# Fused attention and mixture-of-experts kernel: the second scatter of a pair issued without waiting for the first, y held twice, and norm 2 between the two groups of routing scatters

## What is computed

```python
x = alpha * attention_conv(x) + x                      # per image: q, k, v, 1024 x 1024 softmax
t = to_tokens(x)
t = t + proxy_attention(ln(t))                         # cumulative sums over the tokens, 16 proxies
flat = ln(t).reshape(-1, 256)
logits = flat @ gate_w.T                               # (4096, 8)
top_vals, top_idx = top_k(logits, 2)
top_w = softmax(top_vals)
for e in range(8):
    hdn = gelu(flat @ w1[e] + b1[e])                   # (4096, 1024)
    out = out + combine[:, e:e+1] * (hdn @ w2[e] + b2[e])
t = t + out
```

## Time and profile before

| | us |
|---|---|
| median of 3 runs | 944.57 |
| lowest and highest | 942.77, 949.17 |
| the profiled execution | 946.73 |
| its span, first to last instruction | 945.0 |

### The profile page before, as it was taken

The page is one execution under the profiler, slowest core; times in us unless marked ns, Lnnn a source line. Parts: engine busy times, 40 slices in busy tenths (PEclk is TensorE's granted clock), DMA queues, the critical chain, the costliest instruction groups (busy, mean ns, idle before and its releaser), DMA issues.

```text
span 945.0 us, 18862 instructions
## 1 busy us (share of the span) xinstructions
PE 803.9 (85%) x5745; PEld 730.7 (77%) x5746; DVE 481.1 (51%) x1134; ACT 325.0 (34%) x588; POOL 426.8 (45%) x404
## 2 busy tenths in 40 slices
PE   4998789896999999605989989989798986988993
PEld 3888679786566575405989889889798986988993
DVE  4787778685436564332535434544453453444442
ACT  2846557474324342102331332223232323223221
POOL 2564547345115754553435435444444443544422
PEclk9999999998658885656998999989899999999997
DMA  9575765925013231105686676666857777566542
GB/s 305 202 304 195 288 266 162 415 90 225 23 45 67 46 68 51 62 1 179 202 284 205 212 246 190 223 204 217 299 159 240 251 219 263 168 218 195 146 113 24
DMA packets 61043, 171.83 MB, mean 182 GB/s; under 512 B 18017, under 2 KB 48097, under 8 KB 53825
## 3 DMA queue, kind: packets, MB, share of 16 engines
q1 hardware_dynamic: 43632, 146.49, 42.8%
q0 software_dynamic: 16000, 19.48, 11.2%
q10 hardware_dynamic: 1360, 5.24, 1.4%
HBM read 184.23 MB, written 47.78 MB: 246 GB/s over the span
## 4 chain that ended last, share of the span: by engine, by line
DMA 35%; PE 7%; issue 7%; POOL 3%; DVE 1%; POOLq 1%; SPq 0%; DVEq 0%; ACT 0%
DMA out_tok<-y,to_row 34%; PE ps_y L72 2%; PE ps_y L73 2%; PE ps_y L74 2%; POOL x_rows L1184 1%; DVE y L1277 1%; DMA records<-places 1%; PE ps_h L72 1%; PE ps_h L73 1%; PE ps_h L74 1%; POOL out_tok L1190 1%; POOL from_row L1178 0%; POOL to_row L1196 0%; DVE gl L1286 0%; DMA x_rows<-normed,from_row 0%
## 5 line engine op out<-in xcount | busy, mean ns | idle before, releaser
L1239 ACT ACTIVATE g<-ps_h,bias 128x256 f32<-128x256 f32 x288 | 120.7, 471 | 346.7 <-PE ps_h L74 346.7
L72 PE MATMUL ps_y<-wbuf,gl 128*128 x576 | 172.5, 300 | 44.7 <-DVE gl L1286 44.6
L1190 POOL DMA_INDIRECT out_tok<-y,to_row x72 | 120.9, 1679 | 113.9 <-DVE y L1277 77.7
L73 PE MATMUL ps_y<-wbuf,gh 128*128 x576 | 168.9, 293 | 0.0
L74 PE MATMUL ps_y<-wbuf,gh 128*128 x576 | 168.4, 292 | 0.0
L72 PE MATMUL ps_h<-xth,wbuf 128*128 128x256 f32 x576 | 163.2, 283 | 1.4 <-DVE xtl L1263 1.4
L73 PE MATMUL ps_h<-xtl,wbuf 128*128 128x256 f32 x576 | 163.7, 284 | 0.0
L74 PE MATMUL ps_h<-xth,wbuf 128*128 128x256 f32 x576 | 163.0, 283 | 0.0
L72 PEld LDWEIGHTS ps_y<-wbuf,gl 128*128 128x128 f32 x576 | 116.2, 202 | 48.3 <-issue 48.3
L73 PEld LDWEIGHTS ps_y<-wbuf,gh 128*128 128x128 f32 x576 | 116.5, 202 | 0.1
L74 PEld LDWEIGHTS ps_y<-wbuf,gh 128*128 128x128 f32 x576 | 115.9, 201 | 0.0
(11 more groups left out here) (181 smaller groups left out, 1495.3 us busy)
## 6 DMA issues: line engine op xcount, KB each, us to landing
wbuf<-wsplit SPq DMA_DIRECT2D x70, 2048.0 KB, 7.9
wsplit<-wbuf SPq DMA_DIRECT2D x14, 2048.0 KB, 11.4
wraw<-in_w SPq DMA_DIRECT2D x16, 1024.0 KB, 6.5
xraw<-in_x_ch ACTq DMA_DIRECT2D x5, 1024.0 KB, 10.6
tok<-in_x_tok SPq DMA_DIRECT2D x1, 4096.0 KB, 16.9
out_tok<-tok SPq DMA_DIRECT2D x8, 512.0 KB, 4.7
normed<-x SPq DMA_DIRECT2D x8, 512.0 KB, 2.9
x_rows<-normed,from_row POOLq DMA_INDIRECT x72, 4.1
```

Of the source, the lines that this page charges most:

```text
L72: eng.matmul(out, ll, rh, start=first, stop=False)
L73: eng.matmul(out, lh, rl, start=False, stop=False)
L1190: pool.indirect_dma_start(out=out, out_offset=bass.IndirectOffsetOnAxis(ap=to_row[:, half:half + 1], axis=0), in_=y[:, half, :], in_offset ...
L1239: last = act.activation(g[:, f, :], ps_h[:, f, :], ACT.Gelu_apprx_tanh, bias=bias1[:, bass.ds(e, 1), f:f + 1].rearrange("p a f -> p (a f)"))
```

## The change

In stage C `y` and `to_row` are held twice, by the pair's parity. VectorE's `result(u)` waits once, ahead of the bias, for both scatters of pair u-2. GpSimd copies `to_row` first and then waits for the scatters of the pair before; the second half's scatter no longer waits for the first. So that the halves of a pair name no row twice, padding slots now use 256 different tokens: `places` is filled in periods of 256 slots, and `normed` and the output have 256 extra rows in place of 128. The fill of `places` grows from 384 KB to 512 KB, read from a smaller tile.

In stage B the scatters are split by choice: the four of the first choice stand ahead of norm 2, the four of the second behind it.

```diff
-SLOTS = -(-(E * CAP + E * P) // (P * P)) * P * P
+SLOTS = 2 * E * CAP
...
-            pool.iota(no_token[:, :, 0], pattern=[[0, SLOTS // P // P], [1, P]], base=TOK,
+            pool.iota(no_token[:, :, 0], pattern=[[1, PAIR]], base=TOK,
...
-            def scatter(c, par):
+            def scatter(c, par, k):
 
                 wait_apart(pool, record_d, done(c))
-                for k, b in [(k, b) for k in range(2) for b in range(B)]:
+                for b in range(B):
...
                 if exists(i - 1):
-                    scatter(i - 1, 1 - par)
+                    scatter(i - 1, 1 - par, 0)
                 if exists(near):
                     norm2.scale_and_shift(pool, near)
+                if exists(i - 1):
+                    scatter(i - 1, 1 - par, 1)
...
-            def scatter_first(u):
+            def scatter_first(u, par):
+                pool.tensor_copy(to_row[:, par], records[:, bass.ds(u, 1), :, 0].rearrange("p a h -> p (a h)")).then_inc(to_d, 1)
+                wait_apart(pool, to_d, done(u))
                 if later(u, 1):
                     wait_apart(pool, y_out, u * 32)
-                pool.tensor_copy(to_row[:, :], records[:, bass.ds(u, 1), :, 0].rearrange("p a h -> p (a h)")).then_inc(to_d, 1)
-                wait_apart(pool, to_d, done(u))
-                scatter_half(u, 0)
-
-            def scatter_second(u):
-                wait_apart(pool, y_out, u * 32 + 16)
-                scatter_half(u, 1)
+                scatter_half(u, par, 0)
...
-            def result(u):
+            def result(u, par):
                 e = entry(dve, T_EXPERT, u, E - 1)
                 dve.wait_ge(y_mm, done(u))
                 dve.wait_ge(y_d, u * 2 + CREDIT)
+                if later(u, 2):
+                    dve.wait_ge(y_out, (u - 1) * 32)
...
                 for half in range(2):
-                    if later(u, 1):
-                        dve.wait_ge(y_out, (u - 1) * 32 + (half + 1) * 16)
                     dve.wait_ge(yb_d, u * 2 + (half + 1 + CREDIT))
                     share = records[:, bass.ds(u, 1), half, 1].bitcast(F32)
-                    dve.tensor_scalar(y[:, half, :], yb[:, half], share, None, ALU.mult).then_inc(y_d, 1)
+                    dve.tensor_scalar(y[:, par, half, :], yb[:, half], share, None, ALU.mult).then_inc(y_d, 1)
```

More of the change, by code:

```diff
@@ L140, in build @@
     wsplit = nc.dram_tensor("wsplit", [E, P, WROW], F32, kind="Internal").ap()
-    normed = nc.dram_tensor("normed", [TOK + P, C], F32, kind="Internal").ap()
+    normed = nc.dram_tensor("normed", [TOK + PAIR, C], F32, kind="Internal").ap()
     places = nc.dram_tensor("places", [SLOTS, 2], I32, kind="Internal").ap()
@@ L190, in stage_a @@
         wraw = sb("wraw", [P, 2, WROW // 4])
[L191 removed]
+        no_token, zero_row = sb("no_token", [P, PAIR, 2], I32), sb("zero_row", [P, C])
         ps_sc = ctx.enter_context(nc.psum_tensor("ps_sc", [P, N], F32))
@@ L304, in _ @@
             pool.wait_ge(padding_ok, 3)
-            pool.dma_start(places.rearrange("(p g) r -> p (g r)", p=P),
-                           no_token[:, :, :].rearrange("p g r -> p (g r)")).then_inc(record_out[0], 16)
-            pool.dma_start(normed[TOK:TOK + P, :], zero_row[:, :]).then_inc(record_out[1], 16)
+            pool.dma_start(places.rearrange("(n p g) r -> p n (g r)", p=P, g=PAIR),
+                           no_token[:, :, :].rearrange("p g r -> p (g r)").unsqueeze(1).to_broadcast(
+                               [P, SLOTS // P // PAIR, 2 * PAIR])).then_inc(record_out[0], 16)
+            pool.dma_start(normed[TOK:TOK + PAIR, :].rearrange("(h p) d -> p h d", p=P),
+                           zero_row[:, :].unsqueeze(1).to_broadcast([P, 2, C])).then_inc(record_out[1], 16)
             def image(b, more):
@@ L1063, in stage_c @@
         records = sb("records", [P, TILES, 2, 2], I32)
-        from_row, to_row = sb("from_row", [P, SLOT, 2], I32), sb("to_row", [P, 2], I32)
+        from_row, to_row = sb("from_row", [P, SLOT, 2], I32), sb("to_row", [P, 2, 2], I32)
         x = sb("x_rows", [P, SLOT, 2, C])
@@ L1068, in stage_c @@
         gh, gl = sb("gh", [P, FT, PAIR], F32R), sb("gl", [P, FT, PAIR], F32R)
-        yb, y = sb("yb", [P, 2, C]), sb("y", [P, 2, C])
+        yb, y = sb("yb", [P, 2, C]), sb("y", [P, 2, 2, C])
         ps_x = ps("ps_x", [P, KT, PAIR])
@@ L1186, in gather, with scatter_half @@
                                             ).then_inc(x_in[slot], 16)
-            def scatter_half(u, half):
+            def scatter_half(u, par, half):
                 wait_apart(pool, y_d, u * 2 + (half + 1 + CREDIT))
-                pool.indirect_dma_start(out=out, out_offset=bass.IndirectOffsetOnAxis(ap=to_row[:, half:half + 1], axis=0),
-                                        in_=y[:, half, :], in_offset=None, compute_op=ALU.add).then_inc(y_out, 16)
-            def scatter_first(u):
+                pool.indirect_dma_start(out=out, out_offset=bass.IndirectOffsetOnAxis(ap=to_row[:, par, half:half + 1], axis=0),
+                                        in_=y[:, par, half, :], in_offset=None, compute_op=ALU.add).then_inc(y_out, 16)
+            def scatter_first(u, par):
+                pool.tensor_copy(to_row[:, par], records[:, bass.ds(u, 1), :, 0].rearrange("p a h -> p (a h)")).then_inc(to_d, 1)
+                wait_apart(pool, to_d, done(u))
                 if later(u, 1):
                     wait_apart(pool, y_out, u * 32)
-                pool.tensor_copy(to_row[:, :], records[:, bass.ds(u, 1), :, 0].rearrange("p a h -> p (a h)")).then_inc(to_d, 1)
-                wait_apart(pool, to_d, done(u))
-                scatter_half(u, 0)
-            def scatter_second(u):
-                wait_apart(pool, y_out, u * 32 + 16)
-                scatter_half(u, 1)
+                scatter_half(u, par, 0)
             def run(lo, hi):
@@ L1206, in body @@
                     if within(u - 1, lo, hi):
-                        scatter_first(u - 1)
+                        scatter_first(u - 1, (slot - 1) % 2)
                     if within(u + LEAD, lo, hi):
@@ L1210, in body @@
                     if within(u - 1, lo, hi):
-                        scatter_second(u - 1)
+                        scatter_half(u - 1, (slot - 1) % 2, 1)
                 for u in range(lo, min(lo + LEAD, hi)):
@@ L1290, in body @@
                     if within(u - 1, lo, hi):
-                        result(u - 1)
+                        result(u - 1, (slot - 1) % 2)
                     if within(u, lo, hi):
@@ L1395 @@
         args.append(nc.dram_tensor(f"in_{name}", a.shape, mybir.dt.from_np(a.dtype), kind="ExternalInput").ap())
-    out = nc.dram_tensor("out_tok", (TOK + P, C), F32, kind="ExternalOutput").ap()
+    out = nc.dram_tensor("out_tok", (TOK + PAIR, C), F32, kind="ExternalOutput").ap()
     build(nc, *args, out)
```

## The result

The changed kernel takes 880.85 us (median of 4 runs, 863.62 to 909.55; a fifth on record took 885.20), against 946.87 us before (4 runs, 942.77 to 952.06). Two later series of 6 runs gave medians of 860.99 and 874.09 us and ratios of 0.902 (0.896 to 0.909) and 0.911 (0.902 to 0.921). The forecast was 872.0 us, with a range of 862 to 906.

The account below looks back on a forecast made before the run. The prediction took a ring of accumulating scatters and VectorE's y, without TensorE, to bound the kernel. Gains of 66.1 (expert pairs), 3.4 (end) and 3 us (routing) from 946.73, then 2.2 for the median, gave 872.0 us, range 862 to 884.

Parts of the forecast that it names:

- y held twice, second scatter without a wait: Expert stage: scatter waits vanish and pairs take 11.82 us instead of 13.71, 66.1 us less over 35 pairs.
- the sum: 35 pairs at 11.82 us take 413.7 us; whole kernel gains 66.1 + 3.4 + 3 = 72.5 us.
- The lock to the loads: Expert stage: scatters keep step with w1 loads at 11.82 us a pair, scatter 0 leaving 0.34 us before the next load.
- T + 17.7 us is 5 us away in each case: Expert stage: the second scatter lands about 5 us before VectorE needs y, 17.7 us after layer 1 ends (T).
- nothing charged for the w2 loads: Expert stage: second scatter lands 16 to 17 us after T, costing nothing; upper end 1 us for each of 8 experts.
- the ring: GpSimd's cycle of scatter issues, copy, gathers, flight and release: 11.16 us a pair undisturbed, 13.47 with a 6.17 us flight.
- rival B: Expert stage: second scatter's flight averages 5.5 us, 12.8 us a pair, 32 us gained, 906 us in all; chance 0.13.
- A: Expert stage: parallel flights gain little, 13.17 us a pair, 19 us gained there, 919 us in all; chance 0.08.
- C: Expert stage: scatters in flight together delay each other, 15.23 us a pair, slower than before at 991 us; chance 0.03.
- D: Routing stage: norm 1 is late in each step, 10 us lost instead of 3 won, 885 us; chance 0.08.
- The end: Last pair: scatter 1 no longer waits for the first flight, 3.4 us less, all on the path.
- Routing: Routing stage: norm 2 of the last chunk comes earlier; 3 us gained, bounds 8 gained and 10 lost.

Follow-up runs that it names:

- second profile: Profile of the changed kernel, unaltered, in an execution of 849.78 us, from the later series with median 860.99 us.
- the two halves alone: Changed kernel with the second scatter's wait for the first put back, 938.22 us; changed kernel with y held once, 934.23 us.
- `after_third`: Changed kernel, unaltered, run again as base for the kernels beside it: median 874.09 us (854.70 to 889.63, 6 runs).
- first profile: Profile of the changed kernel, unaltered, in its slowest execution, 909.55 us.
- where it was provoked: Changed kernel with one fill of an unused tile on GpSimd ahead of scatter 0 of pair 2: median 884.01 us (4 runs).
- `wait_kept`: Changed kernel with the second scatter's wait for the first put back, y still held twice: 938.22 us (916.10 to 951.20, 4 runs).
- both comparisons of the routing orders: Kernel before with only the routing scatters split, 940.92 against 947.08 us; changed kernel with all eight ahead of norm 2, 884.41 against 874.72 to 879.47.

## Why the prediction was right, and where not

*y held twice, second scatter without a wait.* Right in mechanism and size where nothing tips: 413.7 us for 35 pairs in the second profile is the 413.7 of the sum, with the waits gone and the clock at 1.00. Both edits were needed, which the sum took for granted and the two halves alone showed.

*The lock to the loads.* Right. Scatter 0 leaves about 1.5 us before the next load (forecast 0.34), pair after pair, at 11.82 us. In `after_third` scatter 1 leaves about 4.4 us after the load and flies about 4.9 us, so it lands 9.3 us after the load where I had taken 10.55, and that makes the difference.

*"T + 17.7 us is 5 us away in each case", and nothing charged for the w2 loads.* This is the step that failed. The landing beside a w2 load was right: 504.51 us in the first profile is 16.55 us after its w1 load, forecast 16 to 17. I then let the ring win back time at once. But the next scatter 1 left 0.94 us ahead of a load and flew with it, to 21.2 us after its own load, past the 17.7. From there VectorE waits for the ring (182.3 us), TensorE for VectorE, and the loads for TensorE; over the 35 pairs that makes 12.52 us each. The cost is 24 us in that execution, and 19 us where it was provoked; rival B, at 12.8 us a pair, had the size but a steady cause. It is in one of the three profiles of the changed kernel and, by the estimate above, in 5 of its 17 executions.

*The rivals.* A did not hold: with both scatters in flight a pair takes 11.82 us, not 13.17, and `wait_kept`, which differs by that wait alone, takes 473.30 / 35 = 13.52. The Trainium skill, "DMA: Bandwidth & Descriptors", section "Issuing engines are not separate DMA queues", says of DMAs started on several engines at once that only issue time is saved. I had carried that over to two DMAs of one engine, and for these scatters, whose flights of 3.9 us or more are waited for, it did not come true. C did not occur. D has no run for it: both comparisons of the routing orders point to a gain, neither clear of the spread.

*The end.* From the last matmul to the end of the span are 11.4 us in place of 14.9 (896.27 to 907.7, 930.13 to 945.0): 3.5 us, forecast 3.4.

*Routing.* Forecast 3 us; the medians say 6 and 5 to 10, none of it clear of the spread. The step named was right (norm 2 behind its statistics by 0.1 us). What I left out is that the stage runs at either clock level, which goes with up to 33 us in its length. That a few us of waiting decide how long it stays low, and that the order of the scatters gains by this, is argued, not shown.

*The number.* That 880.85 lies within 9 us of 872.0 is in part luck. By the estimate above two of its four executions lost 13 and 18 us to the ring, and which course routing takes moves a time by tens of us; neither was in the sum. The later medians, 860.99 and 874.09, lie on both sides of the forecast.

## What to carry to other kernels

Where a store's buffer stands in a ring with its flight, count every link of the ring; taking out one may leave a ring that is as long, and two cheap edits together can be worth far more than the sum of each alone (here 42 to 66 us against 6 and 10). A ring that just keeps pace beside large periodic transfers locks to them, and a single delay can cost it a whole period and keep it behind for the rest: look at the least margin between a small transfer's issue and the next large one, not at the mean. Issue small stores whose landing is waited for together and put other issues behind them. Where a time scatters, set it against the granted clock of each execution before you compare medians.

## What the runs showed that I had not expected

- A scatter issued 0.94 us before a 2 MB load flew 10.34 us, where one issued 1.81 us before a load flew 3.9 us.
- One delay of 2.6 us cost 19 us, spread over the 33 pairs from there on.
- The same program had a granted clock of 0.61 or 0.84 in the first 65 us of routing, with TensorE busy for over 90% of them either way. The expert stage began at 409.0 us in one execution and at 444.0 us in another.
